# Routed blocks of a mixture of experts taken in pairs, with their high and low halves made ahead of the transposes

## What is computed

```
x = x + 0.5 * ffn0(layernorm(x))      # 16 experts, top 4, plus a shared expert
x = x + attention(layernorm(x))       # 16 heads of 16, causal, q, k and v normalised
x = x + 0.5 * ffn0(layernorm(x))      # the same weights once more
x = x + 0.5 * ffn1(layernorm(x))      # 32 experts, top 8 cut at a sum of 0.8
x = x + ssm(layernorm(x))             # gated state space layer, 512 inner channels
x = x + 0.5 * ffn1(layernorm(x))
```

```
probs = softmax(x @ gate_w.T); take the top 4, weights cw normalised to a sum of 1
shared = (silu(x @ sg.T) * (x @ su.T)) @ shared_down.T * sigmoid(x @ shared_gate_vec.T)
for each expert e: acc += (silu(x @ wg[e].T) * (x @ wu[e].T)) @ down[e].T * cw[:, e]
ffn0 = shared + acc
```

## Time and profile before

| | us |
|---|---|
| median of 3 runs | 999.32 |
| the profiled execution | 1001.14 |
| its span | 999.3 |
| TensorE busy | 876.1 |
| VectorE busy | 746.2 |
| ScalarE busy | 474.8 |
| GpSimd busy | 424.5 |

### The profile page before, as it was taken

One profiled execution on the slowest core, in us unless ns is written; L12 is line 12 of the kernel. 1 busy time (PEld: TensorE's weight loads), 2 busy tenths in 40 slices (PEclk: granted clock), 3 DMA queues, 4 the chain that ended last, 5 costly groups with the idle time before them and its releaser, 6 DMA issues.

```text
span 999.3 us, 19391 instructions
## 1 busy us (share of the span) xinstructions
PE 876.1 (88%) x6148; PEld 537.4 (54%) x6148; DVE 746.2 (75%) x1636; ACT 474.8 (48%) x981; POOL 424.5 (42%) x402
## 2 busy tenths in 40 slices
PE   4375899999838899979789989899999999999997
PEld 2143665656524566646565546454566545666564
DVE  6777465798888978854886787878878789775554
ACT  4646443467723667534654773235433453332332
POOL 2783037501385522148711987531342324423232
PEclk9778999999959989989999999999999999999999
DMA  9769545433121224665973542121110211112121
GB/s 314 271 202 271 138 137 133 125 83 97 49 75 58 80 50 95 210 172 123 222 180 106 167 148 69 45 76 43 43 53 33 77 43 53 54 40 91 65 73 64
DMA packets 128207, 110.60 MB, mean 111 GB/s; under 512 B 76648, under 2 KB 102888, under 8 KB 128112
## 3 DMA queue, kind: packets, MB, share of 16 engines
q1 hardware_dynamic: 121968, 92.58, 32.1%
q0 software_dynamic: 6144, 16.79, 6.0%
HBM read 58.98 MB, written 34.08 MB: 93 GB/s over the span
## 4 chain that ended last, share of the span: by engine, by line
PE 49%; DVE 8%; issue 4%; POOL 3%; DMA 2%; ACT 2%; POOLq 0%; DVEq 0%; SPq 0%; ACTq 0%
PE ps L1037 21%; PE ps L1081 10%; PE ps L1011 5%; PE ps L1059 3%; PE ps L1224 2%; DVE hid L1295 1%; PE ps L1046 1%; DVE x L1455 1%; POOL wlo L763 1%; DMA xs_sb<-xs_dram 1%; PE ps L1258 1%; POOL back L752 1%; PE ps L1244 1%; POOL hlo L713 1%; PE ps L1234 1%
## 5 line engine op out<-in xcount | busy, mean ns | idle before, releaser
L713 POOL TENSOR_TENSOR hlo<-hid,hhi 128x512 f16<-128x512 f32 x120 | 142.0, 1185 | 269.3 <-ACT hhi L818 268.9
L1295 DVE SCALAR_TENSOR_TENSOR hid<-gtanh,ps 128x176 f32<-128x176 f32 (+1 forms) x244 | 123.4, 506 | 135.8 <-ACT gtanh L801 119.3
L801 ACT ACTIVATE gtanh<-ps 128x176 f32<-128x176 f32 (+1 forms) x244 | 110.1, 451 | 205.2 <-PE ps L1037 160.0
L1037 PE MATMUL ps<-xhi,whi 128*128 128x512 f16 x480 | 185.7, 387 | 20.7 <-DVE hid L1295 19.8
L1037 PE MATMUL ps<-xlo,whi 128*128 128x512 f16 x480 | 185.6, 387 | 0.0
L1037 PE MATMUL ps<-xhi,wlo 128*128 128x512 f16 x480 | 185.4, 386 | 0.0
L1011 PE MATMUL ps<-whi,xs_sb 128*128 x496 | 118.3, 325 | 26.2 <-DVE hid L1311 10.7
L1081 PE MATMUL ps<-whi,hhi 128*128 128x256 f16 x480 | 132.6, 276 | 5.5 <-POOL hlo L713 5.5
L1311 DVE SCALAR_TENSOR_TENSOR hid<-hid,ps 128x176 f32<-128x176 f32 (+1 forms) x244 | 122.8, 503 | 16.9 <-PE ps L1037 11.6
L1081 PE MATMUL ps<-wlo,hhi 128*128 128x256 f16 x480 | 132.4, 276 | 0.0
L1081 PE MATMUL ps<-whi,hlo 128*128 128x256 f16 x480 | 132.2, 275 | 0.0
(11 more groups left out here) (216 smaller groups left out, 1745.5 us busy)
## 6 DMA issues: line engine op xcount, KB each, us to landing
ys_dram<-y_sb SPq DMA_DIRECT2D x124, 128.0 KB
xs_sb<-c_dram SPq DMA_DIRECT2D x64, 192.0 KB, 2.7
scr<-w_in SPq DMA_DIRECT2D x28, 384.0 KB, 4.9
scr<-we_in SPq DMA_DIRECT2D x32, 304.0 KB, 5.2
xs_sb<-c_dram SPq DMA_DIRECT2D x64, 128.0 KB, 2.9
xs_dram<-y_sb SPq DMA_DIRECT2D x2, 3968.0 KB, 16.7
xs_sb<-c_dram SPq DMA_DIRECT2D x64, 64.0 KB, 2.7
scr<-ws_in SPq DMA_DIRECT2D x8, 384.0 KB, 5.2
```

The costliest lines, as they stand in the source:

```text
L713: pool.tensor_tensor(hlo[:, k, :], hid[:, k % 2, :], hhi[:, k, :], ALU.subtract).then_inc(lo_done, 1)
L801: act.activation(gtanh[:, n % 2, 0:w], ps[:, bank, 0:w], ACT.Tanh, scale=0.5 / W_SCALE)\
L1037: mm = pe.matmul(ps[:, bank, :], w[:, off:off + P], a[:, kc, t0:t0 + HN], start=(i == 0), stop=(i == 3 * KC - 1))
L1295: dve.scalar_tensor_tensor(out=hid[:, k, 0:w], in0=gtanh[:, k, 0:w], scalar=1.0, in1=gate, op0=ALU.add, op1=ALU.mult).then_inc(act_done, 1)
```

## The change

- **Pairs.** A routed unit is now two blocks (NRT = 16 units a pass; the last one has one block). Gate and up are two steps as in the shared passes: for each of the two blocks six matmuls of 176 columns into bank 0 (gate) and six into bank 1 (up). tanh, `act`, `h`, the high half and the y copy handle both blocks in one instruction. REGS is 4 pairs of registers, XRING 3 pairs, YRING 2 pairs; a y store writes two blocks, the transposing loads stay one for each block.
- **Halves ahead of the transposes.** ScalarE (`hi`) and GpSimd (`lo`, before on VectorE) split `hid` into a new tile `hp` (two buffers) in f16. TensorE transposes `hp`: four f16 transposes a block: channels 0 to 127 of the high half, 0 to 127 of the low half (of which rows 0 to 111 are used), and channels 112 to 175 of both halves into the upper and the lower 64 rows of one tile. ScalarE copies all of it to `hh` in one instruction (`hT_copy`, 768 columns a pair).
- **Five down matmuls** a block: high x high weights, high x low weights and low x high weights over 112 rows, then the shared 64-row tile: both halves against high weights (laid out twice in the weights) and its high half against low weights.
- **One scatter table.** `xs_dram` serves both halves; it is blanked once, as SyncE's first step ahead of the weights. A routing's sends wait for the last xs loads of the routed pass before.
- **Six gather tiles** (GRING = 6), so a gather step waits for the combine three steps back, not four.
- **No zero fill.** `zero16` and its matmuls go; the first matmul of a pass in each accumulator bank carries the start flag.
- `ORDER` is written anew for all engines. Of GpSimd's string the part around the second routing is shown.

```diff
-IH = I0 // 2
+IA = 112
+IB = I0 - IA
+NRT = -(-NBLK // 2)
-XRING, YRING, GRING = 6, 3, 8
+XRING, YRING, GRING = 3, 2, 6
-REGS = 6
+REGS = 4
-SIZE = {SH: NSH, RT: NBLK, F1: NCH1}
+SIZE = {SH: NSH, RT: NRT, F1: NCH1}
...
             put("PE", "t", "turn", u)
-            put("DVE", "l", "lo", u)
+            put("ACT", "u", "hT_copy", u)
...
-        else:
-            put("PE", "g", "up", u)
-            put("POOL", "l", "lo", u)
+        put("POOL", "l", "lo", u)
+        put("PE", "g", "up", u)
...
         if g == NSH + 1:
-            put("SP", "w", "blank", 0)
-    put("SP", "w", "blank", 1)
+            put("SP", "b", "blank", 0)
...
     "POOL":
-        "A3 w l x2 w x w2 l2 x w l w3 l w l w3 A w5 x4 l3 c2 l c l c l c3 A c A P12 A P c P2 c P c3 A c3 A2 x l "
...
+        "A4 x2 l x l x w l w2 l w2 l w2 l w2 l w2 l w l w2 l2 w l w l w l6 x l x l x l2 x l2 c2 l c l c l2 c A "
...
     "SP":
-        "w30 l6 w6 l2 w2 l w5 l5 y3 l y l y2 l2 y2 l2 y l y l y l y l y2 l2 y2 l2 y2 l2 y l y12 l12 y3 l2 y2 l y "
...
+        "b w21 l w4 l w3 l w3 l w3 l w l w4 l y w2 l y l y l y2 l2 y2 l y l y l2 y7 l6 y l2 y2 l y l y l y l2 y2 "
...
-        xs_dram = [nc.dram_tensor(f"xs_dram{h}", [SLOT_ROWS, 2 * D], F16).ap() for h in range(HALVES)]
+        xs_dram = nc.dram_tensor("xs_dram", [SLOT_ROWS, 2 * D], F16).ap()
...
-        hhi = sb("hhi", [P, 4, HN], F16)
-        hlo = sb("hlo", [P, 4, HN], F16)
+        hh = sb("hh", [P, 4, 2 * HN], F16)
+        hhi, hlo = hh[:, :, 0:HN], hh[:, :, HN:2 * HN]
+        hp = sb("hp", [P, 2, 2, 2, I0], F16)
...
                     if b >= XRING:
-                        sp_.wait_ge(gate_ready, n - XRING + 1)
+                        sp_.wait_ge(up_ready, n - XRING + 1)
...
+                    if PASSES[r][0] == RT:
+                        j, w = (BLOCK[r] + c) % 2, xs_loads(c)
+                        pool.tensor_tensor(hp[:, j, 0:w, 1, 0:I0], hid[:, n % 2, 0:w * I0].rearrange("p (b i) -> p b i", i=I0),
+                                           hp[:, j, 0:w, 0, 0:I0], ALU.subtract).then_inc(lo_done, 1)
...
+                        if q:
+
+                            for k in range(XRING):
+                                pool.wait_ge(xs_loaded[k], 16 * xs_count(RT_PASSES[q - 1], NRT - 1 - (NRT - 1 - k) % XRING))
...
+                elif name == "hT_copy":
+                    r, c = WHERE[n]
+                    w = xs_loads(c) * 3 * P
+                    act.wait_ge(turned, BLOCK[r] + c + 1)
+                    if n >= 4:
+                        act.wait_ge(down_done, n - 3)
+                    act.activation(hh[:, n % 4, 0:w], ps[:, T_BANK, :].bitcast(F16)[:, 0:w], ACT.Copy).then_inc(hT_done, 1)
...
+                        pe.wait_ge(act_done, n)
+                        pe.wait_ge(xs_loaded[c % XRING], 16 * xs_count(r, c))
+                        bank, part, done = G_BANK, 0, gate_ready
+                    else:
+                        pe.wait_ge(h_ready, n)
+                        bank, part, done = U_BANK, I0, up_ready
+                    for j in range(xs_loads(c)):
+                        i = 0
+                        for kc in range(KC):
+                            for w, a in ((whi, 0), (whi, KC), (wlo, 0)):
+                                mm = pe.matmul(ps[:, bank, j * I0:(j + 1) * I0], xs_sb[:, slot + j, a + kc, :],
+                                               w[:, ds(offset[k + j] + (EXP0 + kc * 2 * I0 + part), I0)],
+                                               start=(i == 0), stop=(i == 3 * KC - 1))
+                                i += 1
+                    mm.then_inc(done, 1)
...
-                    pe.wait_ge(h_ready, n + 1)
-                    pe.wait_ge(lo_done, n)
-                    for j in range(2):
-                        mm = pe.transpose(ps[0:IH, T_BANK, P * j:P * j + P], hid[:, n % 2, IH * j:IH * (j + 1)], ident)
+                    m = BLOCK[r] + c
+                    pe.wait_ge(lo_done, n + 1)
+                    if m:
+                        pe.wait_ge(hT_done, m)
+                    hT = ps[:, T_BANK, :].bitcast(F16)
+                    for b in range(xs_loads(c)):
+                        at = 3 * P * b
+                        for out, part in ((hT[:, at:at + P], hp[:, m % 2, b, 0, 0:P]),
+                                          (hT[:, at + P:at + 2 * P], hp[:, m % 2, b, 1, 0:P]),
+                                          (hT[0:IB, at + 2 * P:at + 3 * P], hp[:, m % 2, b, 0, IA:I0]),
+                                          (hT[IB:P, at + 2 * P:at + 3 * P], hp[:, m % 2, b, 1, IA:I0])):
+                            mm = pe.transpose(out, part, ident16[:, :])
...
+                    for b in range(xs_loads(c)):
+                        for i, (part, w, wide, at) in enumerate(((0, whi, IA, 0), (0, wlo, IA, 0), (1, whi, IA, 0),
+                                                                 (2, whi, P, D), (2, wlo, IB, D))):
+                            at_h = P * (3 * b + part)
+                            mm = pe.matmul(ps[:, Y_BANK + m % 2, D * b:D * b + D], hh[0:wide, k, at_h:at_h + P],
+                                           w[0:wide, ds(offset[2 * (n % REGS) + b] + (EXP0 + 2 * KC * I0 + at), D)],
+                                           start=(i == 0), stop=(i == 4))
...
-                        for b in range(2):
-                            pe.matmul(ps[:, ACC + b, :], zero16[:, :], xhi[:, 0, HN * PASSES[r][2]:HN * PASSES[r][2] + HN],
-                                      start=True, stop=False, skip_group_check=True)
...
-                elif name == "lo":
-                    k = n % 4
-                    dve.wait_ge(hi_done, n + 1)
-                    if WHERE[n][1] == 0:
-                        dve.wait_ge(lo_done, n)
-                    dve.tensor_tensor(hlo[0:IH, k, 0:2 * P], ps[0:IH, T_BANK, 0:2 * P], hhi[0:IH, k, 0:2 * P],
-                                      ALU.subtract).then_inc(lo_done, 1)
```

170 lines of the change are left out of this document (81 added, 89 removed), and 102 rows, old and new, of the table ORDER.

## The result

The changed kernel takes 988.74 us (median of 4 runs, 986.87 to 989.24) against 999.86 of the kernel before on the same chip (4 runs, 996.26 to 1001.56): ratio 0.989, 95% interval 0.9859 to 0.9921. It is faster, by 11 us. The forecast was 960, so 28 of its 39 us are missing. The profiled execution took 989.24 us, its span is 987.4, the mean clock 0.974 (before 0.955).

A forecast was written before the change was run, and what follows sets the result against it. TensorE was taken to set the time, through its columns and the 123 us it stands. Terms -15.3 (columns), -10 (gaps), -18 (start), -4 (VectorE), +8 (GpSimd) sum to -39.3, giving 960 us against the median; range 925 to 992, 8 in 10.

The forecast's parts named there:

- The columns: TensorE's matmul work: -11.0 us over 124 routed blocks and -4.3 from the removed zero-fill matmuls, together -15.3 us.
- The rival of small matmuls: TensorE's transposes and 176-column matmuls keep the skill's spacing, about 81 ns at 128 columns: +19, 979 us; chance 0.04.
- Gaps between steps: Routed passes running alone: a pair makes the gate-to-transpose round trip once for two blocks, -10 us (ends 0 and -15).
- columns only: Rival: pairs bounded by their own round trip, start by weights, so only TensorE's columns gain: 984 us; chance 0.17.
- The start: First 100 us: second blanking dropped and first moved ahead of all weights, -18 us (ends +5 and -30).
- The second blanking's -9: Near 78 us: without this 4 MB DMA, tau and the loads behind it no longer queue; 9 us won.
- The first blanking's -9: First 60 us: blanking ahead of the weights delays them, but first send and expert weights no longer wait; -9 us.
- the bound that I had set: Start: a first shared down past 40 us with nothing won later would mean the moved blanking was mispriced.
- VectorE: -4: Routed pass beside the first attention: less VectorE work per block, partly offset by later gathers; -4 us net (+5 to -15).
- GpSimd: +8: GpSimd's in-order queue: routed low halves, later sends and fewer gather tiles +6, shared SBUF interface +2; ends +2, +40.
- The rival with GpSimd as the gate: Sends and gathers delay low halves, TensorE's waits on them grow over 35 us: 1051 in full, 1015 at half; chance 0.12.
- Zero fill: Shared, dense and state-space passes: 20 zero-fill matmuls of 512 columns go, 0.215 us each, -4.3 us within the columns.

## Why the prediction was wrong, step by step

**The columns: -15.3 forecast, +11.9 measured.** This is the failed step, and within it two sentences. "Down: five of 256 instead of six, -0.110": the three 112-row ones do cost 0.11, but the 64-row one and its successor cost 0.21 each, so the part is +0.09 and not -0.11. "Four f16 instead of two f32 ... 0.22, no change": those of 128 columns do take 0.056 to 0.066, but the way into the two of 64 and out of them takes 0.149 and 0.176, which makes 0.39 of it. I priced a matmul by its moving columns alone, and gave the shape of the stationary tile no price. The rows that I read could not show one: they have tiles of 88 rows and of 88 columns beside full ones, and these pay nothing (0.110 apart, 0.150 behind a gate). With the 64s gone, on the one chip where both were traced, TensorE's busy time is 846.6 against 868.8 of the kernel before, -22.2, where the same arithmetic gives -15.3 - 124 x 0.055 = -22.1. So the arithmetic was sound for such shapes; that it agrees to 0.1 is luck, since the kernel before itself varies between traces (868.8 and 876.1). The trace of before had held a warning in another stretch, in the attention, where 64-row tiles alternate with full ones:

```profile
221.25 0.27 PE L1181 MATMUL ps<-scr 64*128 64x256 f16 x1
221.36 0.21 PE L1183 MATMUL ps<-scr 64*128 64x128 f16 x1
221.50 0.29 PE L1186 MATMUL ps<-hide,ident 128*128 128x128 f16 x2
221.72 0.28 PE L1181 MATMUL ps<-scr 64*128 64x256 f16 x1
```

From the 64-row matmul of 128 columns to the full one behind it are 0.15 us and not 0.055, and from the second full one (at 221.57) back to 64 rows again 0.15. I had not looked there. Gate and up were right: matmuls of 176 columns start 0.076 apart, against 0.077.

**The rival of small matmuls.** The Trainium skill, "TensorE: Matmul & The Clock Gate", section "Back-to-back issue gap", gives 81 ns as the sustained spacing of a matmul of 128 columns. For like tiles the runs have 56 ns at 128 columns and 76 at 176, so the rival that I built on it fell; its 979 us were nearer to the result than my 960, for another reason.

**Gaps between steps: -10.** Half in the sum, and not for the reason given. From 475 to 537 it is -6.1, but from 100 to 148 it is +1.0. From 100 to 140 a block took 40 / (198 / 12) = 2.42 us, where before it took 40 / (112 / 6) = 2.14; that is 4.8 a pair, and I forecast 3.5. Of the 2.42 TensorE is busy 2.08, which is the miss of the columns again, and stands 0.34, where before it was busy 1.92 and stood 0.22. So in this stretch a pair covers its round trip no better than two single blocks did, and the sign that I had set for the rival "columns only", over 4.0 us a pair, came. With the shapes alike and four pairs of registers the pace is 40 / (204 / 12) = 2.35; with six pairs it is the same count, but twelve matmuls of 512 columns (2.6 us) fit into the stretch besides. With the registers also loaded early, TensorE stands 1.6 us there ahead of the gates, and 3.9 ahead of the transposes and 2.3 ahead of the down steps. That points at the pair's own round trip; which step of it holds was not found.

**The start: -18.** Half. The second blanking's -9 is confirmed by the run that put it back (9.7). The first blanking's -9 did not come: the stretch to 60 us stands 32.6 instead of 30.2 (31.9 and 32.4 on the other chip with both traces). The first shared down comes at 38.4, within the bound that I had set, but TensorE then stands 10.06 us ahead of the second logits (last line of its timeline above). VectorE is busy there with one instruction; its tile view and GpSimd's timeline of the changed kernel:

```profile
L1386 DVE SCALAR_TENSOR_TENSOR wlo<-scr,whi x23: 778/950/9605, 21.8 to 101.5; 128x608 f16<-128x608 f32 x16, 128x768 f16<-128x768 f32 x7
```

```profile
46.05 0.97 POOL L745 DMA_INDIRECT xs_dram<-xr,pos  x1 [0.30 <-issue]
47.03 1.36 POOL L766 TENSOR_TENSOR wlo<-scr,whi 128x608 f16<-128x608 f32 x1
48.33 1.17 POOL L717 TENSOR_TENSOR hh<-hid,hh 128x512 f16<-128x512 f32 x1
49.44 2.62 POOL L766 TENSOR_TENSOR wlo<-scr,whi 128x608 f16<-128x608 f32 x2
```

An operation of 0.95 us (the median of its 23) took 9.6 while GpSimd ran one operation on two SBUF inputs after another, as in the earlier trace rows. I read it so that with the first weights later, these low halves moved to where the logits wait for VectorE; no run tried it.

**VectorE: -4.** Right in sum: TensorE's standing from 160 to 300 fell from 25.6 to 20.6 us. Its busy time, 701.0, is not the forecast 676. By durations (one chip, both traces) the routed operations give the 70 us back, 69.3, but others grew; 10.8 of it is the product with the combine weights in the dense passes, 965 ns each instead of 853, and these stayed at 964 with the routed low halves off GpSimd. Why they grew stays open.

**GpSimd: +8.** Its busy time, 480.5, is the forecast 482. Its low halves took 0.90 us each as forecast:

```profile
L714 POOL TENSOR_TENSOR hp<-hid,hp 128x352 f16<-128x352 f32 x60 | 53.9, 900 | 99.6 <-ACT hp L818 99.3
```

It stands 99.6 us in front of them, waiting for ScalarE, and TensorE waits only 2.6 us in all for `hp`. The rival with GpSimd as the gate needed over 35. The second routing's sends begin at 129.95 and not by 120. The contention is real, some 11 us of VectorE's durations; how much of it lies on the path was not measured.

**Zero fill: -4.3.** It was not tried alone; matmuls of 512 columns do start 0.216 apart, as priced.

The sum of the terms other than the columns was right (-24 forecast, -23.8 measured), but by luck, through errors that cancel: the start and the gaps each gave half, and the later stretches gave what I had not counted (300 to 450: 17.2 to 11.4 us of standing).

## What to carry to other kernels

A matmul's price was its moving columns as long as the stationary tile had 88, 112 or 128 rows or 88 or 128 columns; each change between these and 64 cost 0.1 us more. Before cutting a contraction into 112 + 64 rows, or a transpose into 128 + 64 columns, look in the trace for rows where the same shapes alternate; full tiles with rows of little use may cost less than fewer rows. Here tiles without a 64 and two more pairs of registers make 0.964 to 0.967 of the kernel before, on chips where the changed kernel makes 0.99. What TensorE saves in work does not all come out as time: of 42 to 45 us of its busy time, 16 to 25 did. And a ratio belongs to the chip that it was taken on: the same change was worth 1.0 to 1.1% on three chips and 2.8% on another.

## What the runs showed of the hardware that was not expected

- A stationary tile of 64 rows or 64 columns between full ones costs TensorE about 0.1 us ahead of it and 0.1 behind it, with 256 moving columns (0.21 between starts instead of 0.11); two such transposes make four take 0.39 us where four alike would take 0.22, though the second of the two starts 0.003 after the first. Two 64-row ones side by side pay nothing between them (0.120). The weight load of the odd tile starts with its own matmul, 0.20 after the one ahead, where like tiles are loaded beside the matmul ahead; what holds both back by 0.1 us the records don't say.
- 112 rows beside 128 rows cost nothing extra (0.11 each), nor do 88 rows or 88 columns (0.110).
- One instruction of VectorE on two SBUF inputs took 9.6 us instead of 0.95 while GpSimd ran such instructions without a pause. The Trainium skill, "GPSIMD Engine Reference", section "1. Specifications", tells of the shared interface; the trace agrees, and shows how large it can be.
- On three of six chips the kernel before takes 3% longer, through stretches beside GpSimd's indirect DMAs in which SyncE's queue moves nothing (read from one trace of such a chip); the changed kernel, on that chip, has no such stretch from 148 to 160. TensorE's clock is lower there as well (0.75 in the stretch from 140 to 165), after it has stood.
